# A fused attention and expert kernel: first q in passes, first scores ahead of V1, expert selection later, batch 0's results earlier

## The chip, the cores and the metric

One core of a Trainium2 chip. The metric is the device time of one execution in microseconds. The profile is of one execution; its span runs from the first to the last instruction.

## What is computed

For x of 2 x 512 tokens with 512 channels (all float32):

```python
xn = layernorm(x)
qkv = silu(xn @ qkv_w.T)            # 32 heads of 128: q, k, v
# linear attention with a decay per head, in blocks of 32 tokens:
scores = (q k^T) * decay            # causal
attn = scores @ v                   # summed over all earlier tokens
normed = norm_w * attn * rsqrt(mean(attn**2 over all heads) + eps)
gate = sigmoid(xn @ gate_w.T)
a = (gate * normed) @ out_w.T
# experts: top 2 of 8 by router, each a rank 16 pair (A, B), and a base layer
e = combine(top2(softmax(xn @ W_router.T)), xn, A, B) * 2 + xn @ W_base.T + b_base
out = x + a + e
```

## The kernel before

**Precision.** Every float32 operand is split in a high part that TensorE reads in its fast float32 form (fp32r, `_hi`) and a low rest (`_lo`). A product is three matmuls: high by high, and each low by the other's high (`three`). ScalarE (ACT) makes the high parts, VectorE (DVE) or GpSimd (POOL) subtracts to get the low ones.

**Products.** The weight products are Strassen products (`product`, m = 1 to 7) on banks p, q, r of PSUM, with the copies and sums `copy_m1`, `make_u2`, `copy_u2`, `copy_u3`, `make_c22`, `make_c12` between them. Product 7 waits for `copy_u2`, that for `make_u2`, that for `copy_m1` of product 1. A unit is one set of seven: V1, V2, QK1, QK2, G23, QK3, QK0, G01, in this order, for four heads. After silu, `hi` and `lo` split a result, and `lo` frees its bank.

**Attention.** `scores(s)` computes one head's triangle in four column blocks, the last one (128x128, plain float32: `k_last`, `q_last`) third; `mask`, `probs01`, `probs_lo01` and their like make the probabilities; `attend(s)` multiplies with v, its last block (`v_last`, `p_last`) at the end. `squares`, `add_square`, `gate_att`, `gated_hi`, `gated_lo` follow, and `output(t)` multiplies a token tile with out_w into `outp`, which `add_out` adds to acc.

**Order.** Each engine's order is written out by hand as a list of calls in `body`: a first pass, a loop of six, a final pass. An engine waits in order, on semaphores; a late instruction holds all behind it.

**Start.** ScalarE makes 24 of the 32 decay tables (`nears`), then the high part of the first chunks of weights (`first_weights_hi(0)`), the high parts of token tiles 0 to 3, the second weights, the other 8 tables, and loads a table of functions. GpSimd makes the low parts (`first_weights_lo`). TensorE turns tiles 0 to 3, does q, k and one gate of batch 0 (`first_rows`), turns tiles 4 to 7 (tile 7 waits for the fourth copy into x_t, since the banks are shared), does the other gate, `router`, and batch 1. The router waits for the x_t copy of tile 4. In the first pass VectorE picks the two best experts (`two_best`) before `make_u2(V1)`, weighs them in place of `add_out(-3)` (`weigh_experts`), and TensorE does `scores(0)` between products 5 and 7 of V1.

**End.** In the final pass G01 and QK0 are the base layer's halves, with the expert products in the same banks (`expert`, `more_experts`). `add_base` adds them to y, which holds x and the bias. `rms` sums the squares into columns, `mean_square`, `power` (GpSimd) and `inverse_root` make the root. `result(t)` of batch 0 is acc times root plus y, by `combined`; for batch 1 ScalarE scales (`scale_part`), GpSimd adds y (`part_result`), and `last_result(t)` adds the last four output tiles (12 to 15), which alternate between `outp` and bank p.

Of the kernel before, what the change touches and what calls it, by code (L numbers as in the profile page):

```python
# [5 lines left out]
F32 = mybir.dt.float32  # L6
# [45 lines left out]
S_ORDER = (0, 1, 3, 2)  # L52
K_COLS = (TB - 1) * P
# [40 lines left out]
def build(nc, x, w_chunks, norm_w, a_router, b_base, slopes, out):  # L94
# [6 lines left out]
    with ctx:  # L101
# [116 lines left out]
        first_whi, first_wlo, first_ready = sem("first_whi"), sem("first_wlo"), sem("first_ready")  # L218
        first_silu, first_high, first_low, first_gate = sem("first_silu"), sem("first_high"), sem("first_low"), sem("first_gate")
        t1_made, t2_made, t3_made, t4_made = sem("t1_made"), sem("t2_made"), sem("t3_made"), sem("t4_made")  # L220
        t_hi_done, t_lo_done, t3_lo_done = sem("t_hi_done"), sem("t_lo_done"), sem("t3_lo_done")
# [39 lines left out]
        def _(sp):  # L261
# [29 lines left out]
            sp.dma_start(ar[:], a_router).then_inc(ar_in, 16)  # L291
            sp.wait_ge(first_wlo, 1)
# [63 lines left out]
            for t in (0, 1, 2, 3, 4, 5, 6, 7):  # L356
                if t < TB:
                    sp.wait_ge(result_done, t + 1)
                else:
                    sp.wait_ge(last_done, t - TB + 1)  # L360
# [9 lines left out]
        def _(pool):  # L370
# [42 lines left out]
            def body(g, first=False, final=False):  # L413
# [28 lines left out]
                def part_result(t):  # L442

                    pool.wait_ge(scaled, t + 1)
                    for c in "rx":
                        pool.wait_ge(free[c], unit(g, QK0 + t // 2) + 1)
                    if t < 2:
                        pool.wait_ge(bias_done[1][0], t + 1)
# [10 lines left out]
                if final:  # L459
# [45 lines left out]
                    add_bias(1, 1)  # L505
                    add_bias(1, 0)
                    add_square(7)
                    power(4, slice(0, 4))
# [31 lines left out]
                low(QK3, 4)  # L540
                add_square(3)
                low(QK0, 1)
# [23 lines left out]
            def first_weights_lo(u):  # L566
                pool.wait_ge(first_whi, u + 1)
                pool.tensor_tensor(first_lo[:, u], raw[u][:], first_hi[:, u].bitcast(F32), ALU.subtract).then_inc(first_wlo, 1)

# [3 lines left out]
            pool.wait_ge(xn_ready, TB)  # L573
            first_weights_lo(0)
            first_weights_lo(1)
# [10 lines left out]
            pool.wait_ge(t_hi_done, 3)  # L586
            pool.tensor_tensor(c_lo[:, 2], t_raw[:, 2], c_hi[:, 2].bitcast(F32), ALU.subtract).then_inc(t3_lo_done, 1)
# [9 lines left out]
        def _(act):  # L597
# [89 lines left out]
            def body(g, first=False, final=False):  # L687
# [76 lines left out]
                if final:  # L764
# [23 lines left out]
                    weight(QK1, 2)  # L788
                    silu(V2, "x")
                    whole(V2, "q")  # L790
                    silu(V2, "q")
                    whole(V2, "x")
                    hi(V2, "q")
                    hi(V2, "x")
                    weight(QK1, 3)
                    whole(V2, "r")
                    silu(V2, "r")
# [54 lines left out]
                    gate(G23, "p")  # L852
                    weight(QK3, 4)
# [286 lines left out]
            for t in range(TB):  # L1140
                tokens_hi(t)
# [1033 lines left out]
```

## Time and profile before

| what | us |
|---|---|
| median of 3 runs | 1096.39 (1094.84 to 1096.84) |
| the profiled execution | 1096.27 |
| its span | 1094.4 |
| TensorE matmul busy | 1075.3 (98%) |
| VectorE / ScalarE / GpSimd busy | 713.3 / 687.5 / 638.6 |
| mean granted clock of TensorE | 0.997 |

A matmul's busy time includes its way through the array, so neighbours overlap; the distance between two starts is what one costs. The clock is a share of 2.4 GHz.

### The profile page before, as it was taken

How to read it: one execution, taken by the hardware profiler on the slowest of the kernel's cores; microseconds unless marked ns; L12 is line 12 of the kernel's file. 1: busy time of each engine (PE TensorE's matmuls, PEld its weight loads, DVE VectorE, ACT ScalarE, POOL GpSimd, SP SyncE). 2: the span in 40 equal slices, each digit the busy share in tenths (PEclk: the TensorE clock that was granted, in tenths of full speed). 3: DMA queues.
4: the chain of work that ended last, by engine and by line, in shares of the span. 5: the costliest groups of instructions: out<-in, count | busy, mean ns of one | idle time of the engine just before them, and what ended most of it. 6: DMA issues, size and time to landing. Idle time of an engine off the chain costs nothing.

```text
span 1094.4 us, 18992 instructions
## 1 busy us (share of the span) xinstructions
PE 1075.3 (98%) x5902; PEld 945.3 (86%) x5902; DVE 713.3 (65%) x1207; ACT 687.5 (63%) x1400; POOL 638.6 (58%) x626
## 2 busy tenths in 40 slices
PE   5999999999999999999999999999999999999998
PEld 5888889888898888988888888988889888998897
DVE  6777575666647576675756667475766757566666
ACT  8577565666667665675756766576666756567631
POOL 5837554484637647376544846367473765548653
PEclk9999999999999999999999999999999999999999
DMA  7203120110201202021111102012020211112222
GB/s 280 83 5 106 37 66 21 45 63 26 63 19 45 75 24 67 0 86 38 48 38 43 62 24 62 19 43 62 24 81 0 81 43 48 39 44 63 63 78 77
DMA packets 41605, 60.04 MB, mean 55 GB/s; under 512 B 3936, under 2 KB 21600, under 8 KB 41568
## 3 DMA queue, kind: packets, MB, share of 16 engines
q1 hardware_dynamic: 40992, 59.01, 17.1%
q10 hardware_dynamic: 576, 0.56, 0.1%
q8 instruction: 20, 0.33, 0.1%
q14 instruction: 17, 0.14, 0.0%
HBM read 52.74 MB, written 6.82 MB: 54 GB/s over the span
## 4 chain that ended last, share of the span: by engine, by line
PE 93%; ACT 2%; DVE 2%; POOL 2%; issue 1%; DMA 0%; ACTq 0%; SPq 0%; DVEq 0%; POOLq 0%
PE bank_q L1793 8%; PE bank_q L1795 8%; PE bank_q L1794 8%; PE bank_p L1793 5%; PE bank_p L1795 5%; PE bank_p L1794 5%; PE bank_r L1793 5%; PE bank_r L1795 5%; PE bank_r L1794 5%; PE outp L1793 5%; PE outp L1794 5%; PE outp L1795 5%; PE att L1793 3%; PE score L1795 3%; PE score L1793 3%; PE att L1795 3%
## 5 line engine op out<-in xcount | busy, mean ns | idle before, releaser
L408 POOL TENSOR_TENSOR w_lo<-combo,w_hi 128x768 fp32r<-128x768 f32 (+1 forms) x128 | 166.8, 1310 | 141.1 <-ACT w_hi L605 140.9
L408 POOL TENSOR_TENSOR w_lo<-raw,w_hi 128x256 fp32r<-128x256 f32 (+1 forms) x128 | 131.7, 1032 | 126.8 <-ACT w_hi L605 126.4
L457 POOL TENSOR_TENSOR sum_sq<-sum_sq,square 128x512 f32<-128x512 f32 x64 | 82.9, 1295 | 79.5 <-ACT square L754 79.5
L1361 DVE TENSOR_TENSOR acc<-acc,outp 128x512 f32<-128x512 f32 x116 | 79.5, 685 | 59.3 <-PE outp L1795 58.3
L1793 PE MATMUL bank_q<-c_hi,w_hi 128*128 128x512 f32 x276 | 109.9, 398 | 0.0
L1795 PE MATMUL bank_q<-c_hi,w_lo 128*128 128x512 f32 x276 | 108.0, 391 | 0.0
L1794 PE MATMUL bank_q<-c_lo,w_hi 128*128 128x512 f32 x276 | 107.7, 390 | 0.0
L1273 DVE TENSOR_TENSOR score<-score,table 128x512 f32<-128x512 f32 (+1 forms) x128 | 75.9, 628 | 42.1 <-PE score L1795 42.1
L605 ACT ACTIVATE p_hi<-score 128x896 fp32r<-128x896 f32 (+1 forms) x128 | 81.2, 649 | 34.8 <-DVE score L1273 33.4
L1793 PE MATMUL outp<-wo_hi,g_hi 128*128 128x512 f32 x252 | 99.6, 395 | 3.2 <-DVE acc L1398 2.8
L1221 DVE TENSOR_TENSOR xs<-bank_r,xs 128x512 f32<-128x512 f32 x64 | 44.2, 691 | 88.9 <-ACT xs L605 61.1
L1794 PE MATMUL outp<-wo_lo,g_hi 128*128 128x512 f32 x252 | 98.8, 392 | 0.0
L1795 PE MATMUL outp<-wo_hi,g_lo 128*128 128x512 f32 x252 | 98.8, 392 | 0.0
L605 ACT ACTIVATE w_hi<-combo 128x768 fp32r<-128x768 f32 (+1 forms) x128 | 81.0, 634 | 19.0 <-PE bank_r L1795 9.8
L605 ACT ACTIVATE xs<-bank_q 128x512 f32<-128x512 f32 x64 | 38.3, 598 | 61.4 <-PE bank_q L1795 61.4
L1215 DVE TENSOR_TENSOR bank_q<-bank_q,xs 128x512 f32<-128x512 f32 x64 | 44.7, 698 | 44.5 <-PE bank_q L1795 24.2
L1793 PE MATMUL bank_p<-b_hi,w_hi 128*128 128x512 f32 x184 | 73.3, 398 | 0.0
L754 ACT ACTIVATE square<-att 128x512 f32<-128x512 f32 x64 | 38.3, 599 | 55.6 <-PE att L1871 55.6
L1795 PE MATMUL bank_p<-b_hi,w_lo 128*128 128x512 f32 x184 | 71.9, 391 | 0.0
L1284 DVE TENSOR_TENSOR p_lo<-score,p_hi 128x896 fp32r<-128x896 f32 x64 | 69.3, 1083 | 3.7 <-ACT p_hi L605 3.7
L1794 PE MATMUL bank_p<-b_lo,w_hi 128*128 128x512 f32 x184 | 71.7, 390 | 0.0
L398 POOL TENSOR_TENSOR combo<-raw 128x256 f32<-128x256 f32 x64 | 48.3, 755 | 39.4 <-DMA raw<-w_chunks 36.6
(277 smaller groups left out, 3481.5 us busy)
## 6 DMA issues: line engine op xcount, KB each, us to landing
raw<-w_chunks SPq DMA_DIRECT2D x165, 256.0 KB, 2.9
near_dram<-near SPq DMA_DIRECT2D x2, 2048.0 KB, 10.1
table<-near_dram SPq DMA_DIRECT2D x32, 128.0 KB, 2.0
y<-x SPq DMA_DIRECT2D x8, 256.0 KB, 3.6
out<-acc SPq DMA_DIRECT2D x7, 256.0 KB, 2.0
acc<-x SPq DMA_DIRECT2D x6, 256.0 KB, 7.6
acc<-x ACTq DMA_DIRECT2D x2, 256.0 KB, 3.9
hw_dram<-acc SPq DMA_DIRECT2D x1, 512.0 KB, 2.8
```

Source lines behind the costliest of these rows:

```text
L398: pool.tensor_tensor(combo[:, 0, :], r[:, 2, :], r[:, 3, :], ALU.add).then_inc(combos, 1)
L408: pool.tensor_tensor(piece(w_lo[i % 2], j), piece_source(i, j), piece(w_hi[i % 2], j).bitcast(F32), ALU.subtract).then_inc(wlo[j], 1)
L457: pool.tensor_tensor(sum_sq[:, s % 2, :], sum_sq[:, s % 2, :], square[:], ALU.add).then_inc(summed, 1)
L605: return act.activation(out_, in_, ACT.Copy, **kw)
L1215: dve.tensor_tensor(bq, bq, xs[:], ALU.add).then_inc(u2_made, 1)
L1221: dve.tensor_tensor(xs[:], br, xs[:], ALU.add).then_inc(c22_made, 1)
L1273: dve.tensor_tensor(score[:, j, 0:P_LEN[j]], score[:, j, 0:P_LEN[j]], table[:, 0:P_LEN[j]], ALU.mult).then_inc(mask01, 1)
L1284: dve.tensor_tensor(p_lo[:, 0:P_AT[2]], score01[:, 0:P_AT[2]], p_hi[:, 0:P_AT[2]].bitcast(F32), ALU.subtract).then_inc(plo01_done, 1)
L1361: dve.tensor_tensor(tile, tile, outp, ALU.add).then_inc(acc_done, 1)
L1793: pe.matmul(out_, a_hi, b_hi, start=start, stop=False, skip_group_check=True)
L1794: pe.matmul(out_, a_hi, b_lo, start=False, stop=False, skip_group_check=True)
L1795: return pe.matmul(out_, a_lo, b_hi, start=False, stop=stop, skip_group_check=True)
```

## The change

1. **First q by passes.** `first_q_rows`: for each half of the tokens all four high by high matmuls, then four with low weights, then four with low tokens, each group with its own wait. VectorE makes the low half for q (`first_qlo`) in place of a part of GpSimd's, and the high part comes in two halves. ScalarE makes 16 tables first, one more after each of two token tiles, 14 later. SP waits for both low halves before it reloads.
2. **Start of the first pass.** `scores(0)` stands before product 6 of V1 instead of behind product 5. Products 7 and 4 carry the waits for the third and fourth low token sums (`t_lo_done`), and VectorE makes the third, which GpSimd made. `first_lows(1)`, `first_gates`, `first_q(1)`, `first_k(1)` and the V2 weights are reordered.
3. **`two_best`** is called at the end of `probs_lo2(0)`, and its last `one_hot` moves into `weigh_experts`.
4. **Attend** takes its blocks in the order 0, 3, 2, 1 (`A_ORDER`).
5. **The final pass.** `rms(0, 0)` stands before output tile 9, `rms(1, 1)` before product 7 of G01. Roots and results of batch 0 come early; the second halves of base are added to acc after the results are made, not to y before. ScalarE scales two tiles before `gated_hi(7)`.
6. Some neighbouring calls of silu, whole, hi, weight, make_c12 and lo change places in every pass.

```diff
+A_ORDER = (0, 3, 2, 1)
...
             sp.dma_start(ar[:], a_router).then_inc(ar_in, 16)
+            sp.wait_ge(first_qlo, 1)
             sp.wait_ge(first_wlo, 1)
...
                 def probs_lo2(s):
...
+                    if first and s == 0:
+                        two_best()
...
-                        dve.wait_ge(y_in[COL[c]][0], 32)
+                        dve.wait_ge(y_in[b][0], 32)
+                        to = y[b][:, 0:2]
                     else:
-                        dve.wait_ge(bias_done[COL[c]][1], 2)
-                    if c == "x":
-                        dve.wait_ge(e_added, u + 1)
+                        dve.wait_ge(part_done if b else result_done, TB)
+                        to = acc[:, TB * b + 2:TB * b + TB]
...
-                    for j in range(TB - 1):
+                    for j in A_ORDER:
...
-                    pe.matmul(att[:, K_COLS:], v_last[r, b][:, e], p_last[:], start=False, stop=True,
-                              skip_group_check=True).then_inc(att_ready, 1)
+                        if j == TB - 1:
+                            pe.matmul(att[:, K_COLS:], v_last[r, b][:, e], p_last[:], start=False, stop=False, skip_group_check=True)
...
                     prod(G01, 1, 6)
                     more_experts(0)
+                    rms(0, 0)
                     output(9)
                     attend(7)
                     more_experts(1)
                     output(10)
-                    prod(G01, 5, 7)
-                    rms(0, 0)
+                    prod(G01, 5)
+                    rms(1, 1)
+                    prod(G01, 7)
                     output(11)
-                    rms(1, 1)
                     prod(G01, 3, 4, 2)
...
+                if first:
+                    scores(0)
                 prod(V1, 6, 1, 5)
-                scores(0)
+                if not first:
+                    scores(0)
                 prod(V1, 7, 2, 4, 3)
...
+            def first_q_rows():
+
+                for half in range(2):
+                    tok = slice(256 * half, 256 * half + 256)
+                    pe.wait_ge(xh_done, 2 * half + 2)
+                    for kc in range(KC):
...
+                    pe.wait_ge(first_qlo, 1)
...
+                    pe.wait_ge(xl_done, 2 * half + 2)
...
-            pe.wait_ge(t_lo_done, 3)
-            pe.wait_ge(t3_lo_done, 1)
+            pe.wait_ge(t_lo_done, 2)
             pe.wait_ge(first_low, TB)
```

**ScalarE at the start**, from the decay tables (near) on; first_hi is the first weights' high part, b_hi the tokens'. Before:

```order
L1088 ACTIVATE near<-diff 128x256 [waits diff_made]
L1088 ACTIVATE near<-diff 128x256 x23
L605 ACTIVATE first_hi<-raw 128x1024 [waits raw_in0]
L605 ACTIVATE b_hi<-score 128x4x128 [waits turned] x2
L605 ACTIVATE b_hi<-att 128x4x128 [waits turned]
L605 ACTIVATE b_hi<-outp 128x4x128 [waits turned]
L605 ACTIVATE first_hi<-raw 128x1024 [waits raw_in1]
L1088 ACTIVATE near<-diff 128x256 x8
L1146 ACTIVATE far<-slope 128x32 [waits slope_in]
```

and now:

```order
L1092 ACTIVATE near<-diff 128x256 [waits diff_made]
L1092 ACTIVATE near<-diff 128x256 x15
L609 ACTIVATE first_hi<-raw 128x512 [waits raw_in0]
L609 ACTIVATE first_hi<-raw 128x512
L609 ACTIVATE b_hi<-score 128x4x128 [waits turned]
L1092 ACTIVATE near<-diff 128x256
L609 ACTIVATE b_hi<-score 128x4x128 [waits turned]
L1092 ACTIVATE near<-diff 128x256
L609 ACTIVATE b_hi<-att 128x4x128 [waits turned]
L609 ACTIVATE b_hi<-outp 128x4x128 [waits turned]
L609 ACTIVATE first_hi<-raw 128x1024 [waits raw_in1]
L1092 ACTIVATE near<-diff 128x256 x14
```

The first weights come after 16 tables instead of 24, in two halves, and two tables stand between the token tiles.

**VectorE in the first pass**, around `two_best`; the operations on sm and h_keep are the selection, bank_q<-bank_q,xs is `make_u2(V1)`, v_lo<-bank_p,v_hi is `lo(V1, "p")`. Before, from the selection's seventh instruction:

```order
L1326 TENSOR_REDUCE sm_1<-sm 128x8 [waits ln]
L1327 TENSOR_TENSOR sm_3<-sm_1,sm_0 128x8 [waits ln]
L1315 TENSOR_TENSOR sm<-sm,sm_1 128x64
L1316 TENSOR_TENSOR sm<-sm 128x64 [waits ln]
L1317 TENSOR_REDUCE sm_2<-sm 128x8 [waits ln]
L1318 TENSOR_TENSOR sm<-sm,sm_2 128x64 [waits ln]
L1215 TENSOR_TENSOR bank_q<-bank_q,xs 128x512 [waits m1_copied,m6_done,ln]
```

and now, around its new place:

```order
L1228 TENSOR_TENSOR xs<-bank_r,xs 128x512 [waits u3_copied,m5_done]
L1295 TENSOR_TENSOR p_lo<-score,p_hi 128x256 [waits phi2_done]
L1332 TENSOR_REDUCE sm_0<-h_keep 128x8 [waits h_kept]
L1324 TENSOR_TENSOR sm<-h_keep,sm_0 128x64 [waits ln]
L1325 TENSOR_TENSOR sm<-sm 128x64 [waits ln]
L1326 TENSOR_REDUCE sm_2<-sm 128x8 [waits ln]
L1327 TENSOR_TENSOR sm<-sm,sm_2 128x64 [waits ln]
L1334 SCALAR_TENSOR_TENSOR sm<-sm,h_keep 128x64 [waits ln]
L1335 TENSOR_REDUCE sm_1<-sm 128x8 [waits ln]
L1336 TENSOR_TENSOR sm_3<-sm_1,sm_0 128x8 [waits ln]
L1243 TENSOR_TENSOR v_lo<-bank_p,v_hi 128x512 [waits high_p]
L1234 TENSOR_TENSOR bank_r<-bank_r,ys 128x512 [waits u2_copied,m3_done]
```

The selection left the front of `make_u2(V1)` for the front of `lo(V1, "p")`.

**VectorE at the end**; the rows on y are `add_base`, acc<-acc,rs,y are results of batch 0, xs<-bank_r,xs is `make_c22(G01)`. Before, from `make_c12(G01)` to the first last result:

```order
L1227 TENSOR_TENSOR bank_r<-bank_r,ys 128x512 [waits u2_copied,m3_done]
L1201 TENSOR_TENSOR rs<-rs 128x4 [waits pow_done]
L1202 TENSOR_TENSOR rs<-rs 128x4 [waits ln]
L1203 TENSOR_SCALAR rs<-rs 128x4 [waits ln]
L1204 TENSOR_TENSOR rs<-rs 128x4 [waits ln]
L1377 TENSOR_TENSOR y<-bank_r,y 128x2x256 [waits bias_done11,c12_made]
L1377 TENSOR_TENSOR y<-bank_q,y 128x2x256 [waits bias_done01,m4_done]
L1377 TENSOR_TENSOR y<-bank_p,y 128x2x256 [waits bias_done01,m2_done]
L1398 SCALAR_TENSOR_TENSOR acc<-acc,rs,y 128x512 [waits free_q,free_p,bias_done00,acc_done,root_done0] x2
L1398 SCALAR_TENSOR_TENSOR acc<-acc,rs,y 128x512 [waits free_p,free_q,acc_done,root_done0] x2
L1398 SCALAR_TENSOR_TENSOR acc<-outp,rs,acc 128x512 [waits last_out,part_done]
```

and now, from the second root:

```order
L1208 TENSOR_TENSOR rs<-rs 128x4 [waits pow_done]
L1209 TENSOR_TENSOR rs<-rs 128x4 [waits ln]
L1210 TENSOR_SCALAR rs<-rs 128x4 [waits ln]
L1211 TENSOR_TENSOR rs<-rs 128x4 [waits ln]
L1228 TENSOR_TENSOR xs<-bank_r,xs 128x512 [waits u3_copied,m5_done]
L1316 SCALAR_TENSOR_TENSOR g_lo<-att,norm_now,g_hi 128x512 [waits ghi_done]
L1370 TENSOR_TENSOR acc<-acc,outp 128x512 [waits out_ready]
L1409 SCALAR_TENSOR_TENSOR acc<-acc,rs,y 128x512 [waits bias_done01,acc_done,root_done0]
L1234 TENSOR_TENSOR bank_r<-bank_r,ys 128x512 [waits u2_copied,m3_done]
L1388 TENSOR_TENSOR acc<-bank_q,acc 128x2x256 [waits result_done,m4_done]
L1388 TENSOR_TENSOR acc<-bank_p,acc 128x2x256 [waits result_done,m2_done]
L1409 SCALAR_TENSOR_TENSOR acc<-outp,rs,acc 128x512 [waits last_out,part_done]
```

Three of batch 0's four results and its root now stand ahead of these rows, and two of base's four additions stand before the first last result instead of all four (one was ahead of the rows of before).

## Rows read from the trace of the kernel before

**Rows 1.** Waits of PE, whole span: who waited for whom, total, times, longest.

```profile
PE score L2064 <- DVE acc L1728: 9.2, 1, 9.2
PE outp L1793 <- DVE acc L1398: 2.8, 1, 2.8
PE bank_p L1793 <- POOL first_lo L568: 2.1, 1, 2.1
PE bank_q L1793 <- ACT ys L605: 1.3, 1, 1.3
```

**Rows 2.** Timeline of PE: start us, us, form, count, idle before it.

```profile
14.90 0.39 PE L1793 MATMUL bank_p<-b_hi,first_hi 128*128 128x256 f32 x1 [2.14 <-POOL first_lo L568]
...
19.34 0.42 PE L1793 MATMUL bank_q<-b_hi,first_hi 128*128 128x512 f32 x1
...
29.49 3.87 PE L2072 MATMUL score<-ar,x_t 128*128 128x136 f32 x32
...
56.04 0.39 PE L1793 MATMUL bank_q<-w_hi,c_hi 128*128 128x256 f32 x1 [1.32 <-ACT ys L605]
...
61.89 0.28 PE L1793 MATMUL bank_p<-w_hi,b_hi 128*128 128x256 f32 x1
```

**Rows 3.** Two stretches: busy time by engine, granted clock, DMA share, GB/s.

```profile
16.10:19.30 3.20, 3.20 (x17) 3.20 (x16) 2.13 (x9) 3.17 (x10) 3.06 (x3) 0.50 1.00 326
1087.60:1091.00 3.40, 3.40 (x14) 2.97 (x13) 0.89 (x2) 0.00 (x0) 0.00 (x0) 0.52 0.51 198
```

**Rows 4.** Landing of the first two weight loads (issued 1.7, 2.1); timeline of ACT.

```profile
L265 SPq DMA_DIRECT2D raw<-w_chunks x2: 423/428/432, 1.7 to 2.1; - x2
...
DMA to landing us min/median/max: 5.2/6.2/7.3
...
3.94 7.46 ACT L1088 ACTIVATE near<-diff 128x256 f32<-128x256 f32 x24
...
25.59 1.21 ACT L605 ACTIVATE b_hi<-score 128x256 fp32r<-128x256 f32 x4 [1.33 <-PE score L2064]
...
27.07 0.60 ACT L605 ACTIVATE x_t<-score 128x512 f32<-128x512 f32 x1
```

**Rows 5.** Timeline of DVE in the first pass, and the idle GpSimd beside it.

```profile
49.21 1.09 DVE L1315 TENSOR_TENSOR sm<-h_keep,sm 128x64 f32<-128x64 f32 x1
...
53.16 0.21 DVE L1315 TENSOR_TENSOR sm<-sm,sm 128x64 f32<-128x64 f32 x1
...
54.66 0.70 DVE L1215 TENSOR_TENSOR bank_q<-bank_q,xs 128x512 f32<-128x512 f32 x1
...
60.45 0.69 DVE L1236 TENSOR_TENSOR v_lo<-bank_p,v_hi 128x512 fp32r<-128x512 f32 x1 [0.96 <-ACT v_hi L605]
...
64.41 0.74 POOL L408 TENSOR_TENSOR w_lo<-raw,w_hi 128x256 fp32r<-128x256 f32 x1 [10.39 <-ACT w_hi L605]
```

**Rows 6.** Timeline of PE near the end: tile 9, and the columns of rms.

```profile
1063.72 0.40 PE L1793 MATMUL outp<-wo_hi,g_hi 128*128 128x512 f32 x1
...
1071.86 0.95 PE L1927 MATMUL score<-ones,sum_sq 128*128 128x1 f32 x8
```

**Rows 7.** Timeline of DVE at the end: a root's operation, four results, the last.

```profile
1078.18 1.18 DVE L1202 TENSOR_TENSOR rs<-rs 128x4 f32<-128x4 f32 x1
...
1082.53 3.89 DVE L1398 SCALAR_TENSOR_TENSOR acc<-acc,rs,y 128x512 f32<-128x512 f32 x4
...
1091.85 0.48 DVE L1398 SCALAR_TENSOR_TENSOR acc<-bank_q,rs,acc 128x256 f32<-128x256 f32 x1 [0.31 <-PE bank_q L1795]
```

**Rows 8.** Timeline of PE: fp32 block last in attend, then inside the scores.

```profile
1040.96 0.38 PE L1871 MATMUL att<-p_end,v_end 128*128 128x128 f32 x2
...
1041.41 0.40 PE L1794 MATMUL score<-q_lo,k_hi 128*128 128x512 f32 x1
...
1042.42 0.38 PE L1853 MATMUL score<-q_end,k_end 128*128 128x128 f32 x2
...
1042.76 0.28 PE L1794 MATMUL score<-q_lo,k_hi 128*128 128x256 f32 x1
```

More of the change, by code:

```diff
@@ L358, in _ @@
                     sp.wait_ge(result_done, t + 1)
+                    if t >= 2:
+                        for c in "pq":
+                            sp.wait_ge(free[c], unit(SGS - 1, G01) + 1)
                 else:
@@ L788, in body @@
                     weight(QK1, 2)
+                    whole(V2, "x")
+                    silu(V2, "q")
+                    whole(V2, "q")
                     silu(V2, "x")
-                    whole(V2, "q")
-                    silu(V2, "q")
-                    whole(V2, "x")
                     hi(V2, "q")
@@ L1180, in _ @@
             first_gates(1, 0)
+            weight(V2, 2)
+            weight(V2, 1)
+            weight(V2, 3)
             first_gates(1, 1)
@@ L1411, in last_result @@
                     dve.wait_ge(part_done, t + 1)
+                    if t >= 2:
+                        for c in "rx":
+                            dve.wait_ge(free[c], unit(g, G01) + 1)
                     for i, cols in enumerate((slice(0, 256), slice(256, HID)) if t == TB - 1 else (slice(0, HID),)):
@@ L1757, in _ @@
             normalise(1)
-            measure(TB)
+            dve.wait_ge(first_whi, 1)
+            dve.tensor_tensor(first_lo[:, 0, 0:2], raw[0][:, 0:2, :], first_hi[:, 0, 0:2].bitcast(F32), ALU.subtract).then_inc(first_qlo, 1)
             for t in range(TB):
                 tokens_lo(t)
-            for t in range(TB + 1, NTB):
+            for t in range(TB, NTB):
                 measure(t)
@@ L2098, in first_rows @@
-                        mm = three(first_bank[r][:, tok], first_hi[:, r // 2, at, w], first_lo[:, r // 2, at, w], hi, lo,
-                                   kc == 0 and part == 0, kc == KC - 1)
+                        pe.matmul(bp[:, tok], first_hi[:, 0, kc // 2, w], b_hi[:, kc // 2, kc % 2, tok], start=half == 0 and kc == 0,
+                                  stop=False, skip_group_check=True)
+                    pe.wait_ge(first_qlo, 1)
+                    for kc in range(KC):
+                        w = slice(kc % 2 * P, kc % 2 * P + P)
+                        pe.matmul(bp[:, tok], first_lo[:, 0, kc // 2, w], b_hi[:, kc // 2, kc % 2, tok], start=False,
+                                  stop=False, skip_group_check=True)
@@ L2100, in first_rows @@
+                    pe.wait_ge(xl_done, 2 * half + 2)
+                    for kc in range(KC):
+                        w = slice(kc % 2 * P, kc % 2 * P + P)
+                        mm = pe.matmul(bp[:, tok], first_hi[:, 0, kc // 2, w], b_lo[:, kc // 2, kc % 2, tok], start=False,
+                                       stop=kc == KC - 1, skip_group_check=True)
                 mm.then_inc(first_ready, 1)
```

179 lines of the change are left out of this document (93 added, 86 removed).

## The prediction

> **What bounds the kernel now.** I read the waits of TensorE over the whole span first, then its rows in order of time around each wait, then the engine that ended the wait, and last the granted clock. Nearly all of the span is matmul work laid back to back, so only TensorE's own waits, and a lower clock, can be won. The waits view [rows 1] has four of more than 1 us: 9.2 us before the first transpose, 2.1 us before the first q product, 1.3 us in V1 of the first pass (bank_q, for the copy into ys), and 2.8 us in the last four output tiles. No wait of over half a microsecond lies between 57 us and 1084 us, so the reordering inside the loop passes has nothing to win. [Rows 2] place the early waits: q starts at 14.90, the first k product at 19.34, the router at 29.49, product 7 of V1 at 56.04 behind its 1.32 us, and V2 at 61.89. [Rows 3] show what a wait costs besides itself: in the 3.2 us from 16.1 and in the 3.4 us from 1087.6 the granted clock is 0.50 and 0.52, the 1.2 GHz level, each time just after one of the two long waits of 2.1 and 2.8 us. At half clock the first stretch does 1.6 us of work in 3.2, the second 1.7 in 3.4. The 1.3 us wait at 54.7 is followed by no such fall.
>
> **q by passes.** The first q product becomes three passes of four matmuls per half: high by high, low weights by high tokens, high weights by low tokens. Same 24 matmuls, same 4.4 us or less [rows 2]. The first pass needs only first_hi and two token tiles. ScalarE makes 16 exponentials instead of 24 first; at 7.46/24 = 0.31 us each they would end at 8.9, but the second transfer of the weights was issued at 2.1 and landed 7.3 us later [rows 4], so first_hi starts at 9.4. Two halves of 0.5 us and the first two token tiles, with one exponential between, then end near 11.9, the fourth tile near 13.4. VectorE is done with the normalising at 11.2 and makes the q low half by 11.9. The transposes end at 12.6; q can follow directly and end near 15.5 instead of 19.34 at the full clock, or 17.7 at half. That looks like 1.6 to 3.8 us.
>
> **Most of it is not kept.** The work of ScalarE is unchanged and it was busy without a pause from 3.94 to 25 us. It now waits 0.5 us for the landing and about 0.7 us in all for transposes, and so reaches the x_t copies 1.2 us later, near 20.4. The transpose of tile 7 needs the fourth of them, now near 23.8, so TensorE, back at the transposes near 21, waits there; they end near 24.3 instead of 26.6. ScalarE then reaches the copies of tiles 4 to 7 at 25.5, where before it waited for the transposes and began at 25.59 [rows 4]: no gain. The router needs the x_t copy of tile 4, done at 27.67 before and about 27.5 now, so it starts near 27.55 for 29.49. That is **1.95 us** gained, with q's clock of no account: 1.5 us later would still be covered by tile 7. From there TensorE has no new wait until the body, which it reaches at 46.05 for 48.0. The DMA queue of SP waits for the two low halves of q's weights one after the other; the later is at 13.1 where it was 14.87, so its V load is no later. Its near tables go out 1.3 us later at worst, and their reader is the next table, over 10 us on.
>
> **Scores ahead of V1.** The wait for c_lo (0.2 us) goes: it is now asked at products 7 and 4. The scores need ScalarE's tanh of the last gate (0.6 us plus the hand-over, so 0.8 us), which product 6 did not. And the scores, 1.8 us, no longer stand between product 5 and product 7. From the end of product 1 the chain to product 7 is a copy, the add `make_u2` of 0.70 [rows 5] and a copy, each copy 0.60 as that of the same size in [rows 4], with hand-overs 2.3 us, and only product 5, 1.44 us, covers it: 0.9 us of wait. Without the selection of experts in front of that add (its row stands at 54.66, behind the selection's) the chain is never later than this. Product 7 starts at 46.05 + 0.85 + 1.83 + 4.32 + 0.9 = 53.95, against 56.04: 2.1 us.
>
> **The selection, moved behind the low probabilities.** Its eight instructions that stay together took 49.21 to 53.2 and a reduction before, some 4.2 us, but they are not all priced alike: the same 128x64 operation took 1.09 us at 49.21 and 0.21 us at 53.16 [rows 5]. At the low price eight with their gaps make 2.0 us. Queued behind them is lo(V1, "p"), which frees bank p for V2. It stood at 60.45 after 0.96 us of idle [rows 5]; now low probabilities end at 57.35, the selection at 59.4, and lo at 60.1. TensorE wants bank p at 53.95 + 5.76 = 59.7, and so starts V2 at 60.15 instead of 61.89. **Start: 1.7 us won.** With the high price it is 62.3, that is 0.4 us lost. I take the low one: before, GpSimd idled for 10.39 us until 64.41 [rows 5], and that idle stretch, some 2 us earlier now, covers the selection's new place, while its old place lay beside GpSimd's combinations. The four further instructions go to the weighing, where VectorE had idle time of its own: nothing.
> The Trainium skill, page "SBUF — State Buffer", section on terms, says that VectorE and GpSimd take a port pair of the memory exclusively and the loser is fully blocked; by that rule, the selection costs 2.0 us beside an idle GpSimd and more beside a busy one, which is what the two prices suggest.
>
> **Attention order.** The plain fp32 block moves from last to second in every attend, 64 in all. As last, from p_end to the second matmul behind it is 1040.96 to 1041.41, 0.45 us; in the scores, where such a block already stands inside, it is 1042.42 to 1042.76, 0.34 us [rows 8]. The difference, 0.11 us, is that between a matmul of 512 and one of 256 columns. So zero; both ends are about 0.01 us x 64 = 0.6 us either way. The swaps of silu, whole, hi and weight in the loop shift work by some 1 us on engines that TensorE does not wait for: zero, as long as that slack holds.
>
> **The tail.** Before, VectorE made the roots late, then added base to four tiles of y and made four results in 3.89 us (from 1082.53), and the third of the last four output tiles had to wait for the last_result behind them: 2.8 us [rows 1]. Now rms(0, 0) stands where tile 9 began, at 1063.72. On the old time line TensorE then does rms 0.8 [rows 6], tile 9 1.5, attend 1.75, experts 0.75, tile 10 1.35, product 5 1.45, rms(1, 1) 0.8, product 7 1.5 and tile 11 1.4, together 11.3, and asks for product 3's input at 1075.0. VectorE gates attend 7 until 1070.0, has the root of batch 0 at 1071.7 (two of its four small operations beside GpSimd's square sum), result(0) at 1072.4, tile 10 at 1073.0, results 1 and 2 at 1074.5, the second root (0.8) at 1075.3 and c22 (0.7) at 1076.0. Three products of 2.2 us, eighteen matmuls each, end at 1082.6, tiles 12 and 13 at 1084.0 and 1085.35. Base q and p are added by 1083.5, last_result(0) by 1084.9, base x and r by 1086.1, last_result(1) by 1086.8. Tile 14 ends at 1086.75 with no wait, tile 15 waits 0.1 and ends at 1088.25. So there is a new wait of 1.05 us, for c22. rms(1, 1) wants the last square sum at 1071.3; GpSimd, with power(4) of 1.0 us put in front, has it at 1071.0. The last VectorE row starts near 1088.45, against 1091.85 [rows 7]: **3.4 us**, made of 2.8 and the 1.7 of half clock, less 1.15 of new waits. Bounds: 4.6 if c22 is not late, 1.7 if the small root operations take 1.18 us as at 1078.18 [rows 7] each time, and c22 slips with them.
>
> **Sum.** 1.7 + 3.4 = 5.1 us. The profiled execution took 1096.27 us with a span of 1094.4; the median of three is 1096.39, so 0.1 above it. The forecast is **1091.3 us**. Within 0.2% (2.2 us) of the time before counts as no change, which is about what a measurement of this kernel can tell.
>
> **Rivals.**
> (1) The selection at its high price, 2.6 us of wait at V2 in place of the 1.3 removed: total 5.1 - 2.1 = 3.0 won, 1093.4 us. For it: most of its rows were dear before. Against: GpSimd's idle. Chance 0.12.
> (2) The clock falls again. The new waits (about 1 us at tile 7, 0.4 at the router; 1.05 at c22) are short but close together; were each group answered by a stretch as in [rows 3], the tail would lose 1.7 and the start at most 1.5 of 3.2: 1094.5 us, no change. Against: the single 1.3 us wait had no such effect. The Trainium skill, page "TensorE: Matmul & The Clock Gate", section "A second HAM failure mode: psum-queue depth-cycling", says frequent short idles between groups can make the clock swing; it would make this rival's time. Chance 0.10.
> (3) Slower: the plain fp32 block, now inside each attend with a 256-column block behind it. If its weight load is exposed there by 0.2 us, 64 times, that is 12.8 us lost and 1091.3 + 12.8 = 1104.1 us. It decides the sign from 5.1/64 = 0.08 us on. Against it stand [rows 8], taken from the very same pattern in the scores. Chance 0.05.
> (4) The start gives nothing at all, because ScalarE, 1.2 us late, does not catch up at the transposes: 1096.4 - 3.4 = 1093.0, or with a tail of 1.7 us 1094.7. Chance 0.08.
> The forecast itself, 0.65, has its own range 1089.5 to 1093.
>
> **Numbers.** Faster: 0.65 + 0.12 + half of (4), 0.81, less 0.01 for the edge at 2.2 us, 0.80. Same: (2) and the other half of (4), 0.14, less 0.01, 0.13. Slower: (3) and those 0.02 for a wait in the loop that I do not see, 0.07. The range reaches from the good ends of both terms (start 3, tail 4.4) to rival (2): 1088.8 to 1094.4.
>
> **What would show it.** Right: the 2.1 and 2.8 us waits gone from the waits view, q from 12.6, the router near 27.5, product 7 near 54, V2 near 60.2, no stretch of half clock after 16 us or at the end, a wait of about 1 us before product 3 of G01, and last_result(1) ahead of tile 14's end. Wrong: q's waits replaced by equal ones at tile 7 and the router; V2 at 62; any new wait that repeats in the loop; or attends longer than before.

## The result, and the profile after

The changed kernel takes **1087.75 us** (median of 6 runs, 1087.27 to 1088.87) against 1096.23 us for the kernel before beside it (6 runs, 1094.84 to 1097.44): the ratio is 0.9926, 95% interval [0.9916, 0.9937], so 8.1 us less by the ratio, 7 to 9 by the interval. The forecast was 1091.3 us, and the range ended at 1088.8. The sign was right, the size was not. One execution of a run below, the attends alone, took 2178.59 us; it is in that run's median of 11 and in no ratio.

The waits of TensorE in the changed kernel, as in [rows 1]:

```profile
PE score L2089 <- DVE acc L1740: 9.2, 1, 9.2
PE score L1807 <- ACT tanh_g L1127: 0.9, 1, 0.9
PE bank_q L1807 <- issue: 0.7, 1, 0.7
PE outp L2089 <- ACT x_t L609: 0.5, 1, 0.5
PE score L2097 <- ACT x_t L609: 0.2, 1, 0.2
```

The 2.1 and 2.8 us waits are gone. The 1.3 us wait in V1 is now 0.7, and the scores wait 0.9 for tanh_g. This view lists none in the loop or at the end; by the distances of the products two small ones are left there, 0.25 us before product 3 of G01 (for c22) and 0.3 before output tile 15. The timeline of TensorE, against [rows 2]: q, its low weights, k, router, scores(0), product 7 of V1, and V2.

```profile
12.50 1.20 PE L2129 MATMUL bank_p<-b_hi,first_hi 128*128 128x256 f32 x4
13.50 0.96 PE L2134 MATMUL bank_p<-b_hi,first_lo 128*128 128x256 f32 x4
...
16.22 0.40 PE L1807 MATMUL bank_q<-b_hi,first_hi 128*128 128x512 f32 x1
...
47.03 0.47 PE L1807 MATMUL score<-q_hi,k_hi 128*128 128x512 f32 x1 [0.89 <-ACT tanh_g L1127]
...
54.10 0.36 PE L1807 MATMUL bank_q<-w_hi,c_hi 128*128 128x256 f32 x1 [0.73 <-issue]
...
60.06 0.39 PE L1807 MATMUL bank_p<-w_hi,b_hi 128*128 128x256 f32 x1
```

V2 starts 1.83 us earlier, and the products from there on 1.9 to 1.95. The stretch of [rows 3] at the start is now at full clock, the 2.4 GHz level:

```profile
16.10:19.30 3.20, 3.20 (x17) 2.61 (x16) 2.09 (x9) 3.18 (x12) 2.84 (x4) 1.00 1.08 384
```

VectorE in the final pass: a root's first operation, results 0, 1 and 2 (x2), c22, result 3, and the last row, against [rows 7].

```profile
1064.80 0.47 DVE L1208 TENSOR_TENSOR rs<-rs 128x4 f32<-128x4 f32 x1
...
1065.92 0.75 DVE L1409 SCALAR_TENSOR_TENSOR acc<-acc,rs,y 128x512 f32<-128x512 f32 x1
...
1067.42 1.43 DVE L1409 SCALAR_TENSOR_TENSOR acc<-acc,rs,y 128x512 f32<-128x512 f32 x2
...
1069.45 0.69 DVE L1228 TENSOR_TENSOR xs<-bank_r,xs 128x512 f32<-128x512 f32 x1
...
1072.94 1.78 DVE L1409 SCALAR_TENSOR_TENSOR acc<-acc,rs,y 128x512 f32<-128x512 f32 x1
...
1082.88 0.48 DVE L1409 SCALAR_TENSOR_TENSOR acc<-bank_q,rs,acc 128x256 f32<-128x256 f32 x1
```

The last row starts at 1082.88 instead of 1091.85: 8.97 us less in these two profiled executions. **Where it came from** is read by laying the two timelines of TensorE over each other and noting how much earlier each product starts. The table gives the start before, after, and the gain so far.

| place | before | after | gain |
|---|---|---|---|
| second product of V2 and after (bank_p, first pass) | 64.98 | 63.03 | 1.95 |
| output tile behind attend(7), first pass | 164.45 | 162.40 | 2.05 |
| the same, second pass | 292.60 | 290.33 | 2.27 |
| third pass | 421.02 | 418.30 | 2.72 |
| fourth pass | 549.87 | 546.23 | 3.64 |
| fifth pass | 678.07 | 674.16 | 3.91 |
| seventh pass | 934.40 | 930.07 | 4.33 |
| output tile ahead of attend(5), final pass | 1037.32 | 1032.77 | 4.55 |
| scores behind attend(5), final pass | 1041.10 | 1036.00 | 5.10 |
| experts' product after that (bank_p) | 1046.53 | 1041.40 | 5.13 |
| last row of VectorE | 1091.85 | 1082.88 | 8.97 |

So the start gave 1.95, the tail 3.84, and the stretch between them, for which the forecast had nothing, **3.2**. It comes in two ways: a slow rise of some 0.2 us in every pass, and steps in the third, fourth and final pass. The rise happens at the attends. Here is one of the 64 attends before, the fp32 block last, and the same in the changed kernel:

```profile
238.71 0.39 PE L1795 MATMUL att<-p_hi,v_lo 128*128 128x512 f32 x1
...
239.83 0.38 PE L1871 MATMUL att<-p_end,v_end 128*128 128x128 f32 x2
239.97 0.47 PE L1793 MATMUL bank_q<-c_hi,w_hi 128*128 128x512 f32 x1
...
240.28 0.40 PE L1794 MATMUL bank_q<-c_lo,w_hi 128*128 128x512 f32 x1
```

```profile
236.51 0.39 PE L1809 MATMUL att<-p_hi,v_lo 128*128 128x512 f32 x1
236.74 0.38 PE L1889 MATMUL att<-p_end,v_end 128*128 128x128 f32 x2
236.88 0.36 PE L1807 MATMUL att<-p_hi,v_hi 128*128 128x256 f32 x1
237.08 0.28 PE L1808 MATMUL att<-p_lo,v_hi 128*128 128x256 f32 x1
...
237.84 0.39 PE L1807 MATMUL bank_q<-c_hi,w_hi 128*128 128x512 f32 x1
238.06 0.40 PE L1808 MATMUL bank_q<-c_lo,w_hi 128*128 128x512 f32 x1
```

The matmul after the fp32 block takes some 0.08 us more to its successor than its like (0.31 for 0.23 with 512 columns, 0.20 for 0.12 with 256), wherever the block stands. From the 512-column matmul in the first row to the last row it is 1.57 us before and 1.55 after. From an attend's first matmul to the fifth behind the attend it is 2.726 us before and 2.700 after (mean of the 64, without the five longest and the five shortest). A pass tells the same: between the output tiles of the table it takes 128.15 us before and 127.93 after where no wait lies in it, 0.22 us for eight attends. No single distance holds the difference; it is spread over several that change by 0.01 us or so, and why they do no run shows.

The steps are waits. Before, in the fourth pass, on VectorE, GpSimd and then TensorE:

```profile
545.56 1.18 DVE L1236 TENSOR_TENSOR k_lo<-xs,k_hi 128x384 fp32r<-128x384 f32 x1
546.66 2.56 DVE L1243 TENSOR_SCALAR table<-table,far 128x128 f32<-128x128 f32 x2
549.14 0.68 DVE L1361 TENSOR_TENSOR acc<-acc,outp 128x512 f32<-128x512 f32 x1
```

```profile
546.27 2.87 POOL L408 TENSOR_TENSOR w_lo<-combo,w_hi 128x768 fp32r<-128x768 f32 x2
```

```profile
549.87 0.50 PE L1793 MATMUL outp<-wo_hi,g_hi 128*128 128x512 f32 x1 [0.42 <-DVE acc L1361]
```

And after, at the same place, VectorE and GpSimd:

```profile
542.50 1.81 DVE L1243 TENSOR_TENSOR k_lo<-xs,k_hi 128x384 fp32r<-128x384 f32 x1
544.24 0.96 DVE L1250 TENSOR_SCALAR table<-table,far 128x128 f32<-128x128 f32 x2
545.12 0.67 DVE L1370 TENSOR_TENSOR acc<-acc,outp 128x512 f32<-128x512 f32 x1
```

```profile
542.05 2.86 POOL L413 TENSOR_TENSOR w_lo<-combo,w_hi 128x768 fp32r<-128x768 f32 x2
```

The two operations of `far_of(4)` (table<-table,far) take 0.96 us together in some passes and 2.56 in others. Each time they take 2.56, 28 times in all traces of this case, they began 0.37 to 0.45 us behind the start of GpSimd's two low parts of 2.87 us, and ended 0.08 or 0.09 us behind the end of these (549.22 and 549.14 here). `add_out(9)` behind them then frees outp late. Before, that is so in the third, fourth and seventh pass (in the seventh just in time for TensorE); after, in the sixth alone, where it does not matter. The last step is the low part of k in the final pass, before:

```profile
1034.01 1.80 DVE L1236 TENSOR_TENSOR k_lo<-xs,k_hi 128x384 fp32r<-128x384 f32 x1 [2.05 <-ACT k_hi L605]
...
1038.79 0.41 DVE L1288 TENSOR_TENSOR p_lo<-score,p_hi 128x256 fp32r<-128x256 f32 x1
```

```profile
1039.30 0.47 PE L1793 MATMUL att<-p_hi,v_hi 128*128 128x512 f32 x1 [0.43 <-DVE p_lo L1288]
```

It stands ahead of the low probabilities and pushes them back; in the changed kernel it stands behind them.

### The profile page after: what moved, and what is told of

Its sections match the earlier page's. It is cut to its first block, busy times and chain, and to the rows that moved or that the text cites. A ratio compares the mean times of both kernels' runs of the same rounds, so it can differ in the third digit from the quotient of the medians.

```text
span 1085.5 us, 18995 instructions
## 1 busy us (share of the span) xinstructions
PE 1071.1 (99%) x5902; PEld 941.5 (87%) x5902; DVE 711.5 (66%) x1209; ACT 686.2 (63%) x1401; POOL 635.4 (59%) x625
## 4 chain that ended last, share of the span: by engine, by line
PE 97%; ACT 1%; DVE 1%; issue 0%; DMA 0%; DVEq 0%
PE bank_q L1807 8%; PE bank_q L1809 8%; PE bank_q L1808 8%; PE bank_p L1807 6%; PE bank_p L1809 6%; PE bank_p L1808 6%; PE bank_r L1807 6%; PE bank_r L1809 6%; PE bank_r L1808 6%; PE outp L1807 5%; PE outp L1808 5%; PE outp L1809 5%; PE score L1809 3%; PE score L1807 3%; PE score L1808 3%; PE att L1807 3%
## 5 line engine op out<-in xcount | busy, mean ns | idle before, releaser
L1807 PE MATMUL bank_q<-c_hi,w_hi 128*128 128x512 f32 x276 | 107.4, 389 | 0.0
L1807 PE MATMUL score<-q_hi,k_hi 128*128 128x512 f32 (+2 forms) x192 | 69.9, 364 | 0.9 <-ACT tanh_g L1127 0.9
```

Source lines behind the costliest of these rows:

```text
L1807: pe.matmul(out_, a_hi, b_hi, start=start, stop=False, skip_group_check=True)
```

## The experiments

Times are medians; the gain is by the ratio to the kernel before on the same chip, with its 95% interval. "Place" times are from each run's own trace. Executions of the kernel before differed by more than one term here: 1091.8 to 1097.0 us of span beside the first four experiments. So sizes under 1 us are taken from the traces.

**One part alone: the attends.** `A_ORDER` and the loop in `attend` that uses it, in the kernel before.

```diff
-                    for j in range(TB - 1):
+                    for j in A_ORDER:
```

> The kernel before with the attention order alone: the plain fp32 block second instead of last in all 64 attends. Theory A (from laying the two traces over each other: each attend moves the later program 0.025 us earlier): 64 x 0.026 = 1.6 us won, 1094.7 us; the three waits of the loop (0.26 at the tile at 421.02, 0.42 at 549.87, 0.43 at 1039.30) stay, so that the waits view still lists att <- p_lo 0.4 and outp <- acc. Rival B: the attend order is all of the 3.1 us that the loop gained, because the faster attends also change those waits: 3.1 us, 1093.1. Rival C, my prediction's term: zero, 1096.2.

1094.56 us (11 runs), ratio 0.9985 [0.9975, 0.9994]: 1.6 us. The gain rises steadily: from an attend's first matmul to the fifth behind the attend it is 2.700 us as in the changed kernel, and a pass takes 127.93. But it was 2.6 us by the final pass in the profiled execution, because the steps at 421 and 549 are won too, though nothing on VectorE was changed: its far_of falls at another moment. The wait for p_lo stays at 0.4. So A for the size per attend, B for a part of the steps; 1.6 us is what 64 attends at 0.026 make, and the interval, 0.7 to 2.7 us, would also hold the 2.6.

**The swaps in the loop alone.**

```diff
-                    lo(QK3, "x")
                     mask(5, 3)
...
                     probs_lo2(5)
+                    lo(QK3, "x")
```

(and the swaps of silu, whole, hi, weight, copy_u2, squares, hw_high, low, make_u2, make_c12 and lo(QK2, "r"), point 6 of the change).

> The kernel before with the swaps of silu, whole, weight, square, lo, make_u2 and make_c12 in the loop alone. Theory A: the three short waits of TensorE in the loop and the final pass go (0.26, 0.6 and 0.5 us on the time line), everything else stays: 1.3 us won, 1094.9 us. Rival B: these waits were chance places of VectorE beside GpSimd, and other such waits come in their place: within 0.4 us, 1096.2. Rival C: the silu ahead of whole lets products start earlier in every pass, over 2 us: but the two traces show no step of that kind outside the attends.

1095.21 us (11 runs), 0.9989 [0.998, 0.9998]: 1.2 us. In the trace the steps are -0.52 at 164.45 (a new wait: far_of at 2.56 in the first pass), +0.27 at 421, +0.31 at 549 and +0.67 at 1041. Only the last belongs to the swaps. Here B is half right: the waits behind far_of move about.

**The start alone, and the tail alone.**

> The kernel before with the changes ahead of V2 alone (first q by passes, scores(0) ahead of V1, selection behind the low probabilities). Theory A: V2 starts 2.0 us earlier as in the changed kernel, and the rest is moved as a whole: 1094.2 us. Rival B: the shift changes how VectorE and GpSimd meet in the loop and brings or takes single waits of 0.3 to 0.5 us: 1093.5 to 1095.0.

1094.17 us (11 runs), 0.9986 [0.9977, 0.9995]: 1.5 us. V2's gain is 1.91 at 64.98, as in the full change, and it is 2.70 in the fifth and sixth pass, with the steps at 421 and 549 won, but 1.75 in the final pass, after a new wait at the seventh and with the wait for p_lo at 0.9. So B as well as A: single waits of half a microsecond come and go with a shift of the whole.

> The kernel before with the changes of the final pass alone (square sums, roots and results of batch 0 early, base added to acc). Theory A: the 2.8 us wait and the half clock at the end go, c22 comes 0.25 us late and tile 15 waits 0.3: 3.8 us won, 1092.4 us. My prediction's term: 3.4 us, 1092.8, with c22 1.05 us late. Rival B: without the shorter start and loop the results fall elsewhere beside GpSimd and c22 is late by over 1 us: 2.5 to 3.0 us won, 1093.5.

1092.37 us (11 runs), 0.9969 [0.996, 0.9979]: 3.4 us. It is theory A's time without its wait: c22 is late here, about as my prediction had it:

```profile
PE bank_r L1803 <- DVE xs L1226: 0.8, 1, 0.8
```

The four parts alone sum to 1.6 + 1.2 + 1.5 + 3.4 = 7.7 us, of 8.1.

**The whole change without the attends.**

> The changed kernel with the plain fp32 block last again in all 64 attends. Theory A: each attend costs 0.025 us more, 1.6 us in all: 1087.75 + 1.6 = 1089.3 us, spread evenly over the passes, with no step. Rival B, single waits of 0.3 to 0.6 us at the output tile behind attend(7) come back with the shifted phase of VectorE and GpSimd: up to 1090.3. Rival C, my prediction's zero: 1087.75.

1089.98 us (5 runs), 0.9943 [0.9929, 0.9956]; against the changed kernel's 1087.75 that is 2.2 us lost (1.9 by the two ratios). In the trace 2.5 us are lost between 65 and 1030 us: the steady loss of 0.02 to 0.03 at each attend, theory A, and waits behind far_of at 2.56 in four passes of seven, rival B.

**Two moves on VectorE that aim at the steps.** The kernel before, with the first move not part of the change:

```diff
+                add_out(9)
                 far_of(4)
-                add_out(9)
```

and `lo(QK3, "x")` behind `probs_lo2(5)` in the final pass.

> The kernel before with two moves on VectorE alone: add_out(9) ahead of far_of(4) in the passes of the loop (not part of the change), and lo(QK3, x) behind probs_lo2(5) in the final pass (one part of the change). Theory A: the waits of 0.26 at 421.02 and 0.6 at 549.87 are far_of taking 2.56 us instead of 0.95 in front of add_out(9), and go, whatever far_of costs; the wait at 1039.30 is the low part of k at 1.80 us in front of p_lo, and goes (0.55 us). Together 1.4 us: 1094.7 us; no step at the output tile behind attend(7) in any pass. Rival B: the waits come from the phase of all engines and turn up elsewhere: within 0.4 us of before.

1093.99 us (11 runs), 0.9979 [0.997, 0.9988]: 2.3 us, of which the trace gives 1.6 to these places. Against the kernel before, the gain steps by 0.26 at 421.02, 0.66 at 549.87 and 0.68 at 1041.10, nowhere else until the last tiles: all six passes between the output tiles behind attend(7) take 128.15 us, where the kernel before has 128.42 and 128.85 in two of them. The fourth pass:

```profile
545.27 1.81 DVE L1236 TENSOR_TENSOR k_lo<-xs,k_hi 128x384 fp32r<-128x384 f32 x1
547.41 0.69 DVE L1361 TENSOR_TENSOR acc<-acc,outp 128x512 f32<-128x512 f32 x1 [0.33 <-PE outp L1795]
548.01 0.96 DVE L1243 TENSOR_SCALAR table<-table,far 128x128 f32<-128x128 f32 x2
```

Theory A holds at each of its three places. The phase of the engines decides in which pass a wait comes, but these two orders on VectorE are what lets it reach TensorE.

This run showed one thing more. It still has the 2.8 us wait at the end, yet the stretch behind it is at full clock, and so is that of the start alone; the attends alone have the half clock in full:

```profile
1084.20:1087.60 3.40, 2.08 (x12) 1.85 (x13) 2.17 (x4) 0.00 (x0) 0.00 (x0) 1.00 0.99 385
```

```profile
1085.00:1089.00 4.00, 4.00 (x14) 3.42 (x14) 0.98 (x3) 0.00 (x0) 0.00 (x0) 0.50 0.44 169
```

(the two moves, then the attends alone). With the same wait, the clock fell in the profiled executions of the kernel before, of the attends alone, of the loop alone and of q alone (below), and not in those of the start alone and the two moves. From the first product of tile 14 to the last row of VectorE it is 4.62, 5.50, 4.62 and 4.63 us in the four and 3.08 in the two. So what I booked at 1.7 us cost 1.5, 2.4 or nothing. That fits the spread of the kernel before: of its 76 executions beside the experiments, seven have a mean granted clock of 1.000 and took 1094.7 us on the mean, the other 69 took 1096.0.

**What brings V2 forward.** Three runs. The changed kernel with the selection of experts at its old place ahead of make_u2(V1):

> The changed kernel with the selection of experts back ahead of make_u2(V1) and its last comparison with it; the first q by passes and scores(0) ahead of V1 stay. Theory A: with scores(0) early there is no idle time of VectorE behind make_u2 to lose, but the selection sits on the chain to product 7 if it runs when it did (49.2 to 53.2 with 1.09 us operations): product 7 starts at 54.1 to 54.5 all the same, since make_u2 stood at 52.67, and lo(V1, p) stands earlier: V2 at 60.1 to 60.5, 1087.7 to 1088.2 us. Rival B, my prediction's view that the new place is what brings V2 forward by 1.7: VectorE reaches the selection at 45 and its operations cost 1 us beside GpSimd's combinations until 51.7, make_u2 starts past 54, and V2 at 61.8: 1089.5 us.

1088.28 us (4 runs), 0.993 [0.9915, 0.9946]. The selection's operations are dear there, from 44.77 to 51.66, and it costs nothing, since VectorE has no other work until 52.62:

```profile
45.01 1.65 DVE L1322 TENSOR_TENSOR sm<-h_keep,sm 128x64 f32<-128x64 f32 x1
...
52.62 0.70 DVE L1222 TENSOR_TENSOR bank_q<-bank_q,xs 128x512 f32<-128x512 f32 x1 [0.95 <-ACT xs L609]
```

```profile
59.87 0.28 PE L1807 MATMUL bank_p<-w_hi,b_hi 128*128 128x256 f32 x1
```

V2 starts at 59.87, 0.19 earlier than in the changed kernel. Theory A holds; the new place of the selection gives nothing. (The trace is 0.9 us longer over the loop by far_of at 2.56 in four passes, so the 0.5 us of the medians need not be the selection's.) Then q by passes alone in the kernel before:

> The kernel before with the first q by passes alone (its high and low weight parts, and its products pass by pass). Theory A: the router ends 2 us earlier, but the selection of experts behind it keeps make_u2 of V1 and V2 at their places, or gives only a part: product 7 of V1 at 55.0 to 56.0, V2 at 60.9 to 61.9, under 1.0 us won, 1095.4 us. Rival B: selection and make_u2 move with the router, and q by passes is all of the start's gain: V2 at 59.9 to 60.1, 2.0 us won, 1094.4 us.

1095.06 us (11 runs), 0.9991 [0.9982, 1.0]. The router is at 27.43 and the last gate products are 1.98 us earlier, but V2 only 0.39:

```profile
61.50 0.28 PE L1797 MATMUL bank_p<-w_hi,b_hi 128*128 128x256 f32 x1
```

Two paths to product 7 take the rest back. One is on VectorE. ScalarE makes q_hi of batch 1 behind GpSimd's combinations, and these, q_hi and VectorE's q_lo are all only 0.35 to 0.38 us earlier than in the kernel before. VectorE goes from q_lo at 46.17 through far_of and the selection with hardly a pause to `make_u2`, which stands 0.41 us earlier than before:

```profile
54.25 0.70 DVE L1218 TENSOR_TENSOR bank_q<-bank_q,xs 128x512 f32<-128x512 f32 x1
```

The other is on TensorE. Product 6 waits for c_lo of the third tile, which GpSimd makes behind its combinations, where that wait was 0.3 before, and the granted clock of the stretch behind it is 0.53, near the 1.2 GHz level:

```profile
PE bank_q L1797 <- POOL c_lo L587: 1.8, 1, 1.8
```

```profile
48.40:52.00 3.60, 3.60 (x20) 3.60 (x19) 3.43 (x7) 0.66 (x2) 3.43 (x5) 0.53 0.31 84
```

From product 6 to the scores it is 5.87 us instead of 4.39 in the kernel before, so the clock takes 1.5 us. Without that, product 7 would still have waited for `make_u2`, and the add for the selection. Theory A holds, and the selection in front of `make_u2` is seen in the trace; c_lo is a second hold that it did not name. And the change without q by passes:

> The changed kernel without the first q by passes. Theory A: the 2.3 us wait of q and the half clock behind it are back, k stands near 19.3 instead of 16.2, the router near 29.4; scores(0) ahead of V1 can't give that back: V2 at 62.0 instead of 60.06, 1087.75 + 1.95 = 1089.7 us. Rival B: the starting stretch is held by something else behind the router, and the loss is under 0.7 us: 1088.3 us.

1090.1 us (6 runs), 0.9942 [0.993, 0.9955], V2 at 61.85, as theory A has it: the other parts alone give 0.04.

```profile
61.85 0.38 PE L1803 MATMUL bank_p<-w_hi,b_hi 128*128 128x256 f32 x1
```

So of V2's 1.83 us, q by passes alone has 0.39, the rest alone 0.04, and both 1.83. They are in series: q moves TensorE's front by 2 us, and the other parts of the start let it through. Which of them does it was not tested one by one. Two things are seen in the trace of the changed kernel: the wait for c_lo is gone, and ScalarE, in its new order, makes q_hi of batch 1 over 8 us earlier, so that VectorE is through with q_lo and far_of by 44.9. Before, then after:

```profile
45.90 0.59 ACT L605 ACTIVATE q_hi<-bank_p 128x512 fp32r<-128x512 f32 x1
```

```profile
37.65 0.59 ACT L609 ACTIVATE q_hi<-bank_p 128x512 fp32r<-128x512 f32 x1
```

**Better than the change?** Product 6 of V1 ahead of scores(0), which waited 0.9 us, and the far_of move:

```diff
                 if first:
-                    scores(0)
-                prod(V1, 6, 1, 5)
-                if not first:
-                    scores(0)
+                    prod(V1, 6)
+                    scores(0)
+                    prod(V1, 1, 5)
+                else:
+                    prod(V1, 6, 1, 5)
+                    scores(0)
```

> The changed kernel with product 6 of V1 ahead of scores(0) in the first pass on TensorE, and add_out(9) ahead of far_of(4) on VectorE. Theory A: the 0.9 us wait of scores(0) for tanh_g is covered by product 6, whose inputs are there by 46.6: 0.5 to 0.9 us won, of which lo(V1, p) gives back up to 0.4: 1087.2 us. Rival B: product 6 has to wait for the low part of its weights on GpSimd (two of them end at 48.6), and the time is lost instead: 1088.5 us or more. far_of alone is expected to give nothing here, since the changed kernel shows no wait there.

1087.21 us (5 runs, 1086.68 to 1087.36), 0.9917 [0.9904, 0.9931]. Product 6 starts at 46.64 after 0.67 us for the low part of its weights on GpSimd, in place of the scores at 47.03 after 0.89; V2 starts 0.41 earlier, the last row stands at 1082.28 for 1082.88. Between A and B: it beats the changed kernel by 0.5 us in the medians, which the intervals don't tell from nothing.

> The changed kernel with product 6 of V1 ahead of scores(0), add_out(9) ahead of far_of(4), and the selection back in VectorE's idle stretch ahead of make_u2(V1). Theory A: of the 0.9 us wait product 6 first kept 0.4; the selection at its old place frees bank p by 58.1, so that V2 starts at 59.5 instead of 59.65: 1087.0 us, 0.1 to 0.2 less than with product 6 first alone. Rival B: the selection's small operations beside GpSimd delay the low part of the weights that product 6 waits for: 1087.4 or more.

1087.47 us (5 runs), 0.9925 [0.9911, 0.9938]; V2 at 59.63 for 59.65. No gain on top, and not by rival B's way either: the wait for the low part of the weights is 0.7 in both.

**Where the fp32 block stands inside the attend.**

```diff
-A_ORDER = (0, 3, 2, 1)
+A_ORDER = (0, 1, 3, 2)
```

> The changed kernel with the plain fp32 block third in every attend (512, 384, fp32, 256) instead of second (512, fp32, 256, 384). Theory A: it matters only that the block isn't the last thing of the attend, so that the matmul behind it is one of the attend's own: same time, 1087.75 us, and each attend as long within 0.005 us. Rival B: the gain hangs on what stands in front of it (a block of 512 columns): behind one of 384 columns half or all of the 0.025 us per attend is lost, 0.8 to 1.6 us over the kernel: 1088.6 to 1089.4 us. Single waits of 0.26 us at the output tile behind attend(7) may come or go with the phase, in either case.

1087.75 us (6 runs, 1086.48 to 1088.4), 0.9928 [0.9915, 0.994], equal to the changed kernel's. B is out. In the trace a pass without a wait is even shorter, 127.71 us for 127.93, though some output tiles behind attend(7) wait again, and the last row is at 1082.04, 0.84 us earlier. Whether the third place is better stays open; the medians don't show it.

## Why the prediction was right and wrong

- **Start, 1.7 forecast, 1.95 measured.** q follows the transposes (12.50 for "from 12.6"), but k starts at 16.22 and not 15.5: q's first matmuls came slower, at 0.25 us apart. That this is of no account was right. (ScalarE was without a pause to 24.3 before, not to 25 as I had it; it changes nothing.) Router 27.43 for 27.55, scores' wait 0.89 for 0.85, product 7 at 54.10 for 53.95, its wait 0.73 for 0.9, V2 at 60.06 for 60.15: each row within 0.2 us. The waits at tile 7 and the router, which I had near 1 and 0.4 us, are 0.5 and 0.2. The low price of the selection (0.21 to 0.23 us each, 57.45 to 59.40) was right too. The number is right; the part that I credited is not: I held the selection's new place to be what keeps the 1.7 us, and with the selection back V2 starts 0.19 us earlier still. I had priced the old place by the old time line, where VectorE came to the selection at 48.97 and make_u2 stood right behind it. In the changed kernel VectorE has nothing to do from 44.9 to 52.7, and the selection fits in there even at its high price. And "the wait for c_lo (0.2 us) goes" was far too small a price: behind an earlier router it is 1.8 us, with 1.5 us of lower clock behind it.
- **Attention order, zero forecast, 1.6 us measured alone (1.7 in the pair of traces).** I compared two matmuls only, 0.45 with 0.34 us, and set their difference against one of 512 and 256 columns. That hid a gain which is spread over many matmuls: 0.016 us per attend at the second matmul behind it, 0.026 at the fifth. My bound of 0.01 us per attend was the reading error of one row, not of 64 places with the same sign, and I left even its 0.6 us out of the range. This step failed: a term set to zero that measured 1.6.
- **The swaps in the loop, zero forecast, 1.2 us measured alone.** "No wait of over half a microsecond lies between 57 us and 1084 us, so the reordering inside the loop passes has nothing to win" was the second step that failed. Two waits of 0.42 and 0.43 us stood below my threshold, their whole effect on the timeline was 0.66 and 0.68, and a third of 0.26 was in no list. Together 1.6 us. Of these only the wait of 0.43, 0.68 on the timeline, is the swaps' own (lo(QK3, "x") behind probs_lo2(5)); the other two went in the changed kernel as they did with the attends alone, by far_of falling at another moment.
- **Tail, 3.4 forecast, 3.84 measured in the pair of traces, 3.4 with the tail alone.** c22 was to be late by 1.05: 0.8 with the tail alone, and some 0.25 with the whole change, where the first root's operations took 0.47, 0.17, 0.17 and 0.16 us. Tile 15 waits 0.3 for 0.1. Half clock is gone; in the pair of traces it was worth 1.5 and not 1.7. These three differences, 0.8 more, 0.2 and 0.2 less, make the 0.4 us over the forecast.
- **Rivals.** (1) did not come: all eight at the low price. (2) did not come: the granted clock is 1.00 from 16.1 on and at the end. By the rule quoted beside it, of the Trainium skill, page "TensorE: Matmul & The Clock Gate", section "A second HAM failure mode: psum-queue depth-cycling", short idles close together may make the clock swing; here four of 0.2 to 0.9 us between 23 and 54 us did not. (3) did not come; the sign was the other way. (4) did not come.

The terms with their measured sizes add up: 1.95 + 1.7 (attends) + 0.9 (far_of) + 0.55 (low part of k) + 3.84 = 8.9, against 8.97 in the traces. The forecast was too small by the three terms in the middle, 3.2 us; with them at zero even the good ends of its start and tail, 3 and 4.4 us, end at 1089.0.

## What to carry to other kernels

A list of waits with a threshold is no bound: small waits that repeat, and costs that show as no wait at all, are found by laying two timelines over each other at the same products, or before a change by adding up equal places. A change of 0.02 us in something that is done 64 times has the same weight as a wait of 1 us: price it from several places and over a few instructions on either side. And do not give a gain to the part that seems to have been in the way: here two parts gave 0.39 and 0.04 us alone and 1.83 together, and the selection's new place, which I had credited, gave nothing.

## What the runs showed of the chip that I had not expected

- The same pair of 128x128 operations on VectorE takes 0.96 or 2.56 us at the same place of different passes. Where the low part of k directly in front of it took 1.8 us or more, the pair took 0.96; where that took 0.55 to 1.2, the pair took 2.56 and ended 0.08 us behind GpSimd's two low parts, in all 28 cases. So there it is GpSimd's end that decides when the next operation of VectorE comes. The Trainium skill, page "SBUF — State Buffer", section "Terms", says VectorE and GpSimd lock a shared port pair and the loser is fully blocked; the two levels agree with that, and no run here shows the port itself.
- After the same 2.8 us wait, the granted clock fell to its lower level in four profiled executions and stayed at 1.00 in two, of kernels with the same tail. After the 1.8 us wait of q alone it fell to 0.53, after the 1.3 us wait of the kernel before it did not.
- The granted clock of a profile can miss such a stretch. In the change without q by passes it reads 1.00 from 16.1 to 19.3, yet three matmuls of 256 columns take 0.64 us there up to 18.0 and 0.36 behind it; the distance of the matmuls is the surer sign.
- The matmul behind a plain fp32 block takes 0.08 us more to its successor, with 512 as with 256 columns.
